# Four-batch decoder layer on one core: zero products at the start, later gate steps, smaller first placing sets, last results scattered to token rows

## The reference

```python
x = x + causal_attention(layernorm(x))              # one head, width 128
x = x + cross_attention(layernorm(x), ctx, mask)    # 16 heads of 8, 154 keys
x = x + ffn(layernorm(x))
# ffn: 16-head self-attention with rotary positions, then
x1 = layernorm(y + attn_out, g1, be1)
comb = top-2 of softmax(x1 @ Wg + bg) over 8 experts, renormalised
h  = gelu(x1 @ W1[e] + b1[e]);  z = h @ W2[e] + b2[e]      # 128 -> 512 -> 128
out = layernorm(x1 + sum_e comb[e] * z[e], g2, be2)
```

## Time and profile before

| | us |
|---|---|
| median of 3 runs | 706.97 |
| the 3 runs | 704.19, 706.97, 717.64 |
| profiled execution | 712.63 |
| its span in the trace | 710.8 |
| PE busy in the span | 628.3 (88%) |
| DVE busy | 457.2 (64%) |
| ACT busy | 347.3 (49%) |
| POOL busy | 121.2 (17%) |

### The profile page before, as it was taken

One profiled execution on the slowest core, in us unless ns is written; L12 is line 12 of the kernel. 1 busy time (PEld: TensorE's weight loads), 2 busy tenths in 40 slices (PEclk: granted clock), 3 DMA queues, 4 the chain that ended last, 5 costly groups with the idle time before them and its releaser, 6 DMA issues.

```text
span 710.8 us, 11259 instructions
## 1 busy us (share of the span) xinstructions
PE 628.3 (88%) x4110; PEld 394.7 (56%) x4118; DVE 457.2 (64%) x1119; ACT 347.3 (49%) x617; POOL 121.2 (17%) x121
## 2 busy tenths in 40 slices
PE   4899899998898999999898999999899999779940
PEld 2564454446655664378636744478546644468930
DVE  4673588937934878557827768677627698387214
ACT  0415126873044458765154558764336488534510
POOL 5100200001050200011223300030406000310423
PEclk9999999999989999999899989999999999997975
DMA  6400000001043540004251640011353600138751
GB/s 200 116 0 1 1 0 2 1 1 38 1 154 99 154 145 1 1 1 120 87 165 46 181 114 1 1 49 50 104 160 116 192 22 1 30 97 249 224 130 41
DMA packets 45086, 55.00 MB, mean 77 GB/s; under 512 B 4346, under 2 KB 35432, under 8 KB 45032
## 3 DMA queue, kind: packets, MB, share of 16 engines
q1 hardware_dynamic: 43240, 50.61, 24.5%
q0 software_dynamic: 1792, 3.67, 1.6%
HBM read 46.73 MB, written 7.54 MB: 76 GB/s over the span
## 4 chain that ended last, share of the span: by engine, by line
PE 61%; DVE 22%; issue 5%; POOL 4%; ACT 4%; DMA 3%; SPq 1%; POOLq 0%; DVEq 0%; ACTq 0%
PE banks L1775 10%; PE banks L1761 6%; PE banks L1406 4%; PE banks L1420 4%; PE banks L1740 4%; PE banks L1382 3%; DVE nm L1173 3%; PE banks L1722 3%; DVE hat L927 3%; PE banks L1657 2%; PE banks L1655 2%; PE banks L1674 2%; PE banks L1668 2%; POOL yg L632 2%; POOL rstd L600 2%
## 5 line engine op out<-in xcount | busy, mean ns | idle before, releaser
L1237 DVE TENSOR_REDUCE nm<-banks 128x1 fp32r<-128x512 f32 x256 | 160.4, 684 | 28.6 <-PE banks L1740 24.0
L880 ACT ACTIVATE px<-banks 128x1024 f32<-128x1024 f32 x128 | 128.7, 1025 | 30.2 <-PE banks L1761 28.4
L600 POOL TENSOR_TENSOR rstd<-ve,misc 128x4 f32<-128x4 f32 x19 | 19.5, 1026 | 437.1 <-DVE ve L921 437.1
L708 ACT ACTIVATE hT<-banks,wp 128x128 f32<-128x128 f32 x216 | 61.6, 370 | 64.8 <-PE banks L1406 64.7
L1775 PE MATMUL banks<-px,vf 128*32 128x256 f32 (+1 forms) x832 | 78.4, 449 | 2.8 <-ACT px L880 1.2
L1740 PE MATMUL banks<-kst,qst 32*128 32x512 f32 x256 | 77.6, 502 | 1.6 <-ACT kst L853 0.8
L1406 PE MATMUL banks<-xT,wp 128*128 128x128 f32 x432 | 60.7, 285 | 8.5 <-DMA wp<-in_experts 5.5
L1406 PEld LDWEIGHTS banks<-xT,wp 128*128 128x128 f32 x432 | 54.5, 196 | 15.7 <-issue 9.5
L1420 PE MATMUL banks<-wp,hT 128*128 128x128 f32 x432 | 58.7, 279 | 2.1 <-ACT hT L708 2.1
L1761 PE MATMUL banks<-q2st,kst 32*128 32x512 f32 x256 | 59.6, 502 | 0.1
L1420 PEld LDWEIGHTS banks<-wp,hT 128*128 128x128 f32 x432 | 53.6, 194 | 3.5 <-ACT hT L708 2.7
(11 more groups left out here) (278 smaller groups left out, 1043.8 us busy)
## 6 DMA issues: line engine op xcount, KB each, us to landing
wp<-in_experts SPq DMA_DIRECT2D x54, 514.0 KB, 4.2
b2r<-in_L_ffn_b SPq DMA_DIRECT2D x60, 64.0 KB, 4.0
px<-in_experts SPq DMA_DIRECT2D x6, 514.0 KB, 4.8
expert_rows<-xs SPq DMA_DIRECT2D x12, 256.0 KB, 4.3
xs<-expert_tokens SPq DMA_DIRECT2D x9, 256.0 KB, 2.9
msk<-in_mask SPq DMA_DIRECT2D x4, 308.0 KB, 3.2
xin<-in_x SPq DMA_DIRECT2D x4, 256.0 KB, 2.9
ot<-in_const_sel SPq DMA_DIRECT2D x1, 1024.0 KB, 5.1
```

Of the source, the lines that this page charges most:

```text
L708: ins = act.activation(hT[:, n % 2, c * P:(c + 1) * P], bank[h_bank(p, i)][:, c * P:(c + 1) * P], ACT.Gelu, bias=weights(n, 2 * FF + c, 2 ...
L880: act.activation(px[:, c % 2, 2 * i:2 * i + 2, :], banks[:, 4 + 2 * i:6 + 2 * i, :], ACT.Exp, scale=SCALE_H).then_inc(k["f_exp"], 1)
L1237: dve.tensor_reduce(nm[:, t, g, BLK * hh:BLK * hh + 1], bank[s1_bank(g, t, i)], AX.X, ALU.max, negate=True).then_inc(k["f_max"], 1)
```

## The change

It has these parts. (a) PE multiplies zeros (seven 128x512 products of `kbd`, right after it is cleared) before its first wait, POOL's later memsets wait until the first normalised rows (`hat1`) are written, and a run of `keep_warm` has 13 products instead of 8. (b) In `cross`, gate steps 16 to 24 stand behind the 16 maxima: 16 to 19 ahead of the `q2st` copies, 20 to 24 behind the `ktail` copies. `turn_tokens` of group 0 stands ahead of `turn_heads`. (c) The last batch's first group is placed in two sets of two tiles (256 columns); the second set's products follow `up(0)`. (d) b2 rows of the last two groups go to a part of `vf`, with no wait for `y_out`. SP issues the store of the batch before's last group ahead of the loads of tiles 4 to 7. (e) The last batch's results are not stored by slot and gathered by token. DVE splits the slots in two parts and forms `noted`; POOL scatters the token's row number to `slot_rows` (`send_ids`, eight DMAs); SP loads it as `row_of`; POOL scatters each tile of results to its token's row (`send_rows`, 15 DMAs), and SP loads whole rows for the mixing. (f) The last three tiles' biases are added one tile at a time, in two banks in turn, and the last normalisation is split in two fused passes and two output DMAs.

```diff
+PLACES = ((0, 2), (2, 4), (4, 8), (8, 12), (12, NT))
+PLACE_BANKS = (1, 2, 4, 1, 2)
+PLACES_BEHIND = {0: 1, 2: 2, 5: 3, 9: 4}
...
-GATE_AT = ((1, 2), (3, 4), (5, 6), (7, 8), (9, 10), (11, 12), (13,), (14,), (15,), (), (16, 17), (18, 19), (20, 21),
-           (22, 23), (24,), ())
+GATE_AT = ((1, 2), (3, 4), (5, 6), (7, 8), (9, 10), (11, 12), (13,), (14,), (15,), (), (), (), (), (), (), ())
+GATE_BEHIND = ((16, 17, 18, 19), (20, 21, 22, 23, 24))
...
+def b2_place(n):
+
+    return n % 2 if n < NG * B - 2 else 2 + n % 2
+
+
...
+            place = YG * b2_place(n)
+            if place < 2 * YG:
+                return b2r[:, place + first:place + last, :]
+            return vf[:].rearrange("p t h c -> p (t h c)").rearrange("p (j d) -> p j d", d=D)[:, place - 2 * YG + first:place - 2 * YG + last, :]
...
-                if g >= 2:
+                if g >= 2 and b2_place(g) < 2:
...
-                    if done % YG == 0:
+                    if done % YG == 0 and p < B - 1:
...
                         load_expert(B - 1, i)
                     keep_y(p, NG - 2)
+                    keep_y(p, NG - 1)
                     for i in range(YG, WSLOTS + WMORE):
                         load_expert(B - 1, i)
-                    keep_y(p, NG - 1)
-                else:
+                    sp.wait_ge(k["xs_sent"], 16 * 2 * T * B)
+                    sp.dma_start(row_of[:], row_dram.rearrange("(s i) o -> s (i o)", s=P)).then_inc(k["slots_loaded"], 16)
+                elif p < B - 1:
...
+            sp.wait_ge(k["out_stored"], 16 * (B - 1))
+            for i in range(2):
+                sp.wait_ge(y_sent[i], 16 * sum(min(YG, NT - YG * g) for g in range(i, NG, 2)))
+            for t in range(T):
+                sp.dma_start(yg[:, :, t, :], yt_dram[0:2 * S].rearrange("(j t p) d -> p j t d", j=2, p=P)[:, :, t, :],
+                             ).then_inc(xs_in[t], 16)
+            for i in range(2):
+                sp.wait_ge(k["out_ready"], B - 1 + 2 * (i + 1))
+                sp.dma_start(out[B - 1].rearrange("(t p) d -> p t d", p=P)[:, 2 * i:2 * i + 2, :],
+                             outb[:, 2 * i:2 * i + 2, :]).then_inc(k["out_stored"], 16)
+            sp.wait_ge(k["out_stored"], 16 * (B + 1))
...
+            pool.wait_ge(k["ln_hat0"], T)
...
+                pool.wait_ge(k["g_noted"], 1)
+                pool.wait_ge(k["xs_zeroed"], 32)
+                for j in range(2 * T):
+                    pool.indirect_dma_start(row_dram, bass.IndirectOffsetOnAxis(noted[:, j:j + 1], 0),
+                                            row_ids[:, j:j + 1], None).then_inc(k["xs_sent"], 16)
...
+                if i == 0:
+                    pool.wait_ge(k["slots_loaded"], 32)
+                if i % YG == 0 or g == NG - 1:
+                    pool.wait_ge(k["y_out"], n + 1 + i % YG * (g == NG - 1))
+                pool.indirect_dma_start(yt_dram, bass.IndirectOffsetOnAxis(row_of[:, i:i + 1], 0),
+                                        ysb[:, n % 2, i % YG, :], None).then_inc(y_sent[g % 2], 16)
...
-            pool.wait_ge(k["g_slots"], B)
+            send_ids()
             fetch_tokens(B - 2)
+            for i in range(YG):
+                send_rows(i)
             finish(B - 2)
-            fetch_tokens(B - 1)
+            for i in range(YG, NT):
+                send_rows(i)
...
+                    if p == B - 1 and g >= 2:
+                        dve.wait_ge(y_sent[n % 2], 16 * YG)
...
+            def add_last_biases():
+
+                n = NG * B - 1
+                dve.wait_ge(b2_in[b2_place(n)], 16 * b2_loads(n))
+                dve.wait_ge(y_sent[n % 2], 16 * YG)
+                for j in range(NT - YG * (NG - 1)):
+                    dve.wait_ge(k["y_part"], NT * (B - 1) + YG * (NG - 1) + j + 1)
+                    dve.tensor_tensor(ysb[:, n % 2, j, :], bank[last_y_bank(j)][:, j * D:(j + 1) * D],
+                                      biases(n, j, j + 1)[:, 0, :], ALU.add).then_inc(k["y_out"], 1)
...
+                if p >= 0:
+                    for i in GATE_BEHIND[0]:
+                        gate_step(p, i)
...
+                if p >= 0:
+                    for i in GATE_BEHIND[1]:
+                        gate_step(p, i)
...
+                first, last = PLACES[i]
+                g = first // YG
+                at = slot_at[:, g, :] if g else slot_f[:]
+                columns = slice(P * (first - YG * g), P * (last - YG * g))
...
+            own.inc(dve.tensor_scalar(slot_parts[:, 0, :], slot[:, (B - 1) % 2, :], P - 1, None, ALU.bitwise_and))
+            own.inc(dve.tensor_scalar(slot_parts[:, 1, :], slot[:, (B - 1) % 2, :], 7, None, ALU.logical_shift_right))
+            own.wait()
+            dve.scalar_tensor_tensor(noted[:], slot_parts[:, 0, :], float(NT), slot_parts[:, 1, :], ALU.mult,
+                                     ALU.add).then_inc(k["g_noted"], 1)
+            for g in range(1, NG):
+                own.inc(dve.tensor_scalar(slot_at[:, g, :], slot_f[:], -float(S * g), None, ALU.add))
+            own.wait()
             for label in LAST_GAPS[:4]:
                 add_biases(B - 2, label)
-            place_tokens(1)
+            place_tokens(2)
             for label in LAST_GAPS[4:]:
                 add_biases(B - 2, label)
-            place_tokens(2)
             place_tokens(3)
-            add_biases(B - 1, (0,))
+            place_tokens(4)
+            add_biases(B - 1, (0, 1))
             end_step(B - 2, 0)
-            add_biases(B - 1, (1,))
             end_step(B - 2, 1)
             end_step(B - 2, 2)
-            add_biases(B - 1, (2, 3))
+            add_biases(B - 1, (2,))
+            add_last_biases()
             end_step(B - 1, 0)
             end_step(B - 1, 1)
-            end_step(B - 1, 2)
-            dve.wait_ge(k["end_hat"], T * B)
-            dve.tensor_tensor(outb, outb, bc(VEC_G2), ALU.mult).then_inc(k["end_scaled"], 1)
-            dve.wait_ge(k["end_scaled"], B)
             dve.wait_ge(k["x2b_ready"], B)
-            dve.tensor_tensor(outb, outb, x2b[:, (B - 1) % 2], ALU.add).then_inc(k["out_ready"], 1)
...
+            own.wait()
+            for t in range(T):
+                own.inc(dve.scalar_tensor_tensor(yg[:, 0, t, :], yg[:, 0, t, :], mean[:, 4, t:t + 1], vecs[:, VEC_G2, :],
+                                                 ALU.subtract, ALU.mult))
+            dve.wait_ge(k["ln_rstd4"], B)
+            own.wait()
+            for t in range(T):
+                dve.scalar_tensor_tensor(outb[:, t, :], yg[:, 0, t, :], rstd[:, 4, t:t + 1], x2b[:, (B - 1) % 2, t, :], ALU.mult,
+                                         ALU.add).then_inc(k["out_ready"], 1)
...
+            zeros = kbd[:].rearrange("p g h k -> p (g h k)")
+            pe.wait_ge(k["zeroed"], 1)
+            for _ in range(7):
+                pe.matmul(bank[7], zeros[:, 0:P], zeros[:, P:P + S], start=True, stop=True)
...
+                at = y_bank(p, g)
+                if p == B - 1 and g == NG - 1:
+                    at = last_y_bank(i % YG)
+                    if i % YG:
+                        pe.wait_ge(k["y_out"], NG * p + g + i % YG - 1)
                 pe.wait_ge(k["h_act"], n + 1)
...
+                if p >= 0:
+                    turn_tokens(p, (0,))
...
-                    turn_tokens(p, (0,))
+                    turn_tokens(p, (1,))
                 project_heads(n, 0, wx[:, 3, :], 4)
                 if p >= 0:
-                    turn_tokens(p, range(1, NG))
+                    turn_tokens(p, range(2, NG))
...
-                keep_warm(8, 6)
+                keep_warm(13, 6)
```

More of the change, by code:

```diff
@@ L125 @@
 N_EARLY_LOADS, N_SEL_LOADS = 4 + 6, 3
-N_LOADS = 9 + 8
+N_LOADS = 10 + 8
 NT = (2 * S + NE * (P - 1)) // P
@@ L364, in build @@
         slot = sb("slot", [P, 2, 2 * T], I32)
+        row_ids = sb("row_ids", [P, 2 * T], I32)
+        row_of = sb("row_of", [P, NT], I32)
+        slot_parts = sb("slot_parts", [P, 2, 2 * T], I32)
+        noted = sb("noted", [P, 2 * T], I32)
         xs = sb("xs", [P, NT, D])
@@ L429, in weights, with biases @@
             return px[:].rearrange("p i h s -> p (i h s)")[:, first:last]
+        def biases(n, first, last):
+            place = YG * b2_place(n)
+            if place < 2 * YG:
+                return b2r[:, place + first:place + last, :]
+            return vf[:].rearrange("p t h c -> p (t h c)").rearrange("p (j d) -> p j d", d=D)[:, place - 2 * YG + first:place - 2 * YG + last, :]
         def a_scores(t):
@@ L1335, in place_tokens @@
                         own.wait()
-                    ins = dve.scalar_tensor_tensor(placing[g][:, t, :], slot_no, slot_at[:, g, T + t:T + t + 1],
-                                                   placing[g][:, t, :], ALU.is_equal, ALU.add)
+                    ins = dve.scalar_tensor_tensor(placing[g][:, t, columns], slot_no[:, columns], at[:, T + t:T + t + 1],
+                                                   placing[g][:, t, columns], ALU.is_equal, ALU.add)
```

(4 more changed lines are left out.)

100 lines of the change are left out of this document (59 added, 41 removed).

## The result

| | before | after |
|---|---|---|
| median of the runs | 705.74 us (4 runs) | 695.51 us (4 runs, 695.09 to 695.64) |
| ratio, 95% interval | | 0.9861 [0.9834, 0.9888] |
| profiled execution | 712.63 us, span 710.8 | 695.6 us, span 693.7 |
| mean granted clock | 0.958 | 0.970 |

The account below looks back on a forecast made before the run. PE, busy 88% of the span, left only its waits, its lower clock level and the end to gain. 712.6 - 2.2 - 5.7 - 5.8 - 5.1 = 693.8 us, stated as 694, range 685 to 702.

Parts of the forecast that it names:

- (a) The opening: Kernel start: projections 0.6 us earlier, zero products 0.6, longer keep_warm run 1.0; 2.2 us gained, from 0.6 to 3.6.
- the unread products: Longer keep_warm run ahead of the query projection at 33.63: less idle time, 1.0 us gained (0 to 1.1).
- (b) Gate steps: Cross stages of batches 1 to 3: seven maxima take 5.0 us instead of 7.0; 1.9 us gained each, 5.7 in all.
- The cover of 3.5 us: Cross stages: token loads land by 214.5, PE asks for group 0 near 218, so the later scatter costs nothing.
- The clock: Cross stages: two stages of 2.9 us at the lower level saved against the profiled execution, 5.8 us; lower end none.
- (c) Placing sets: Last batch's first group: two sets of 256 columns delay the bias addition and tile 1's weights; 1.9 us lost at up(1).
- (d, e) Order and scatters: Last batch: no b2 load waits, weights of tiles 8 to 14 there by 672; eleven scatters at 1.26 us set the end.
- (f) The end: After the final loads: last output leaves at 703.0 against 708.13, 5.1 us less, the placing sets' loss included.
- The clock falls all the same: Rival, cross stages: the 5.8 us of lower clock stay, or half of them; 697 to 700 us, chance 0.25.
- GpSimd's queue gives the end back: Rival, last batch: 0.3 us more on each of eleven scatters, as much again in fetch and finish; 699 to 702, chance 0.1.
- More at the front and the end: Rival: zeros hold the clock (1.3 us more), placing sets lose nothing (1.9), median one slow stage below profile; 688, chance 0.22.
- The slow rival: Row-number scatter delays SP's row_of load and tiles 8 to 14's weights; gain of 18.8 us used up from 680; chance 0.03.

Follow-up runs that it names:

- steps_only: The kernel before with one edit, gate steps 16 to 24 of batches 1 to 3 moved behind the row maxima; 698.54 us, ratio to before 0.9807.
- steps_back: The changed kernel with only the gate steps put back between the maxima; 707.64 us, ratio to before 0.9976.
- one_set: The changed kernel with the first placing set whole again (four tiles, 512 columns); 696.93 us, ratio to before 0.9863.
- rows_first: The changed kernel with rows of tiles 4 to 7 sent before batch 2's power, and batch 2's last two passes on DVE; 689.95 us, ratio to before 0.9747.
- sqrt_act: The changed kernel with the last power taken from GpSimd, as DVE's reciprocal and ScalarE's square root; 694.68 us, ratio to before 0.9780.
- weights_ahead: The changed kernel with SP loading the last batch's tiles 0 to 3 weights ahead of their bias rows; 695.29 us, ratio to before 0.9825.
- bias_first: The changed kernel with DVE's last two bias additions of batch 2 between the first and second placing sets; 722.04 us, ratio to before 1.0036.
- best: The changed kernel with the edits of bias_first, rows_first, sqrt_act and weights_ahead together; 712.28 us, ratio to before 0.9911; run again, 713.82 us, 0.9920.
- the last two sets: Runs beside before: bias_first, best and best with the old opening (722.04, 712.28, 714.78 us), then best again (713.82 us).

## Why the prediction was right, step by step

**(a) The opening, 2.2 us: not there in the profiled execution, 0.9 in the means of the traces, in the start of the projections.** They started at 10.68, as said (10.7), 0.6 us earlier than before; by 33.84 that was lost again (33.63 before). The mis-sized terms are the two that rest on the clock: the zeros bought nothing for the projections (3.78 us again, and 3.63 to 3.78 in all fourteen traces) and the unread products 0.1 us at 33.84 (1.98). That step took a share of something that comes or doesn't, and the fourteen traces scatter over 3.6 us for it. The granted clock doesn't tell the level there: in 8 to 16 it reads 1.00 before and 0.63 after, for the same 3.78 us.

**(b) Gate steps, 5.7 us: right, 6.1.** Seven maxima took 5.03 us against 7.01 in batch 1, and the `q2st` copies waited 0.40. The late scatter began at 199.89 (200 predicted) and the loads at 211.18 (211.5). The cover of 3.5 us was wrong: PE asked for the tokens at 213.8, not near 218, since the stage's own gain of 4.9 us, the clock's share with it, brings the asking forward while the loads go back. The rows landed just then and PE waited 0.26 us (0.24 in batches 2 and 3), so there was no cover left.

**The clock, 5.8 us: mechanism right, size 8.6.** Two stages kept 3.0 us each (4.98 and 5.05 less 2.0), and a third low stretch of before, 0.57 in 418 to 426 of batch 2's self-attention, was missing too: 2.6 us. I had read the clock only where the diff stood. The window in the trace of before:

```profile
418.00:426.00 8.00, 7.81 (x54) 2.43 (x50) 5.22 (x9) 4.45 (x5) 0.00 (x0) 0.57 0.00 1
```

`steps_only` and `steps_back` show the cause for the cross stages; the third stretch goes and comes with the same edit, but is argued: `steps_only` lacks it, and in `steps_back` a low stretch begins at the same 418.7 as in before, though it lasts 41 us there. Why a self-attention some 70 us behind the moved steps should feel them, no run shows.

**(c) Placing sets, 1.9 us lost at `up(1)`: right, 1.7** (12.43 against 10.73 us behind the slots; before's two instructions are below), but what of it could be told by `one_set` doesn't reach the end. The terms as written, 5.6 - 4.4 + 0.8 - 0.4, make 1.6 and not 1.9. The loss was counted on the path; the path ran over the stores and GpSimd's queue.

```profile
634.34 0.17 DVE L1144 CAST slot<-slot_f 128x8 int32<-128x8 f32 x1
...
645.07 2.05 PE L1406 MATMUL banks<-xT,px 128*128 128x128 f32 x8 [0.58 <-DMA px<-in_experts]
```

**(d, e) Order and scatters: right.** Counted from the slots, the row of eleven scatters was to begin 43.8 us later and began at 45.0; it ran at 1.28 us each (12.76 / 10) without a gap; the first mixing was to come at 61.4 and came at 62.3. PE's one wait for weights behind tile 4 was 0.68 us, at 652.65. `rows_first` shows that this queue, not PE, is the end's bound.

**(f) The end: the step that failed.** The last output was to leave 68.7 us behind the slots and left at 69.5. From there the prediction took before's 2.7 us to the end. It took 4.9, since GpSimd's drain behind the power was now the last thing to finish; `sqrt_act` showed it, by taking 2.2 us off. So the whole end gave 2.1 us in place of 5.1: 0.8 went in the steps ahead, 2.2 in the drain. The term was taken from a place where two paths ended within 0.3 us of each other, and only the visible one was moved.

**Sum.** -2.2 became +0.1, -5.7 became -6.1, -5.8 became -8.6 with 0.4 more on the way to the last slots, and -5.1 became -2.1: 17.1 us of span, 712.6 to 695.6 as times, where 693.8 was worked out. That the sum came so near is partly luck, since terms that were 5.3 us too large met others 3.6 too small. Against the median the luck is greater: the clock's 8.6 us are in the profiled execution of before, which lay 5.7 us over the median of three and 6.9 over that of four (705.74), so the median fell by 10 us and not by 13.

**Rivals.** "The clock falls all the same" is out: no low stretch in the three stages. "GpSimd's queue gives the end back" was right in place and wrong in kind: the scatters kept their pitch, and the engine's last act cost 2.2 us. "More at the front and the end" did not come (the 2 us of `one_set`'s opening show that its first half could have). The slow rival did not come in the changed kernel; its hold on SP is there in `one_set`, `weights_ahead` and `bias_first`, 2.0, 3.9 and 7.2 us. Its sum left out the slack it names: the load may land at 661 and is wanted at 666, so the 18.8 us are used up at 685, not 680.

## What to carry to other kernels

Small steps set between the reductions that feed the matmul engine cost their own time, 2 us a stage here, and can cost the clock on top, 3 us more; put them where the engine has products queued. Before you credit a shorter end, look at each engine's closing drain: the engine whose drain is long (here GpSimd's, 5.75 to 7.02 us behind its last instruction) should have nothing left to do near the end. And when several engines share a late stretch, find the one queue that feeds the end; here a wait of 5 us taken from PE gave 2.4, and by way of GpSimd's queue, while 6.0 came from filling that queue's own gap.

## What the runs showed of the hardware

- GpSimd's closing drain took 7.02 us from the issue of its last instruction (7.02 to 7.03) in each of the eight traces whose kernels scatter their results and end with the power, and 5.75 us in the two with before's end. With a scatter as its last instruction (`sqrt_act` and the three of `best`) it ended 6.8 us behind that scatter's start. What makes it 1.27 us longer than before's wasn't tried. The closing drains of PE, DVE and ScalarE took 0.2 to 2.1 us.
- A scatter of 128 elements of 4 bytes costs GpSimd no less than one of 128 rows of 512 bytes: eight took 10.9 us, 1.36 each (625.63 to 636.5; 11.6 in four other traces), and eleven of the others 13.7, 1.25 each.
- ScalarE's square root of four columns took 0.20 us and DVE's reciprocal 0.18, against GpSimd's power of 1.09. The square root's table load, 1.28 us, stood 19 us ahead of it, where ScalarE had nothing else to do.
- Waits that the trace calls "remote", with SP rows of almost no length beside them, stood only in the four traces of the last two sets, up to 10.8 us long; their cause is open.
- The lower clock level came and went from trace to trace in the opening. In the cross stages it never came once the steps were moved: in all twelve such traces, those of the last two sets too, the three stages take 45.7, 48.7 and 48.4 us from the `ot` copy ahead of them to their first one, within 0.1 us; in before it is 50.7, 53.8 and 50.4.
